# Criss-cross attention on one core: the second pair of channel tiles takes rows first and columns second, with a head of 30 projection pieces and no turn

## What is computed

```python
q = einsum('bchw,oc->bohw', x, Wq) + bq      # 64 channels, k alike
v = einsum('bchw,oc->bohw', x, Wv) + bv      # 512 channels
eH = einsum('bchw,bcpw->bhwp', q, k)         # column strip, diagonal masked with -inf
eW = einsum('bchw,bchp->bhwp', q, k)         # row strip
att = softmax(concat([eH, eW], 3), 3)
outH = einsum('bcpw,bhwp->bchw', v, att[..., :H])
outW = einsum('bchp,bhwp->bchw', v, att[..., H:])
out = gamma * (outH + outW) + x
```

## Time and profile before

| | |
|---|---|
| median of 3 runs | 4426.95 us (4395.76 to 4439.74) |
| the profiled execution: time, span | 4430.1 us, 4428.3 us |
| share of the span in which PE, DVE, ACT, POOL are busy | 80%, 58%, 42%, 28% |
| mean granted TensorE clock, as a share of full | 0.86 |
| moved by DMA | 1179.35 MB, mean 266 GB/s |

### The profile page before, as it was taken

One profiled execution on the slowest core, in us unless ns is written; L12 is line 12 of the kernel. 1 busy time (PEld: TensorE's weight loads), 2 busy tenths in 40 slices (PEclk: granted clock), 3 DMA queues, 4 the chain that ended last, 5 costly groups with the idle time before them and its releaser, 6 DMA issues.

```text
span 4428.3 us, 97049 instructions
## 1 busy us (share of the span) xinstructions
PE 3545.5 (80%) x33624; PEld 2431.6 (55%) x33624; DVE 2586.0 (58%) x3802; ACT 1875.7 (42%) x3852; POOL 1246.6 (28%) x1075
## 2 busy tenths in 40 slices
PE   3987978778887887878977798878988778884865
PEld 1544755456564564645655466554755456563755
DVE  6546764477554774538745576455765477554643
ACT  1545634165241752427532474325634165242621
POOL 0000341404413044220433214240241404413333
PEclk9998799888898798997999879889799888996665
DMA  7958688986989779996899968899689986999399
GB/s 273 297 187 276 209 275 263 326 279 197 312 259 315 255 200 307 289 315 224 240 303 310 302 206 257 273 325 292 208 272 268 330 280 194 316 261 286 96 288 287
DMA packets 824051, 1179.35 MB, mean 266 GB/s; under 512 B 56560, under 2 KB 574192, under 8 KB 823536
## 3 DMA queue, kind: packets, MB, share of 16 engines
q1 hardware_dynamic: 509136, 831.94, 61.5%
q10 hardware_dynamic: 314400, 340.86, 24.0%
HBM read 832.83 MB, written 339.74 MB: 265 GB/s over the span
## 4 chain that ended last, share of the span: by engine, by line
issue 33%; DMA 26%; PE 21%; POOL 10%; DVE 4%; SPq 3%; ACT 2%; ACTq 1%; POOLq 0%; DVEq 0%
DMA xr<-x 23%; POOL acc L496 4%; PE banks L1033 4%; PE banks L1034 4%; PE banks L1035 4%; POOL prob_col L486 4%; PE banks L1107 3%; PE banks L1109 2%; PE banks L1108 2%; DMA v_in<-v_pixel_major 2%; POOL qk_pair L468 2%; SPq L377 1%; DVE floor L770 1%; PE banks L1085 1%; DMA x_first<-x 1%
## 5 line engine op out<-in xcount | busy, mean ns | idle before, releaser
L1033 PE MATMUL banks<-wv_hi,x_hi 128*128 128x512 f16 x2304 | 936.2, 406 | 247.9 <-DVE x_lo L804 247.8
L812 DVE SCALAR_TENSOR_TENSOR v_out<-banks,proj,v_out 128x512 f16<-128x512 f32 x576 | 431.2, 749 | 1076.7 <-ACT v_out L591 1075.8
L496 POOL TENSOR_TENSOR acc<-acc,xr 128x768 f32<-128x768 f32 x384 | 716.3, 1866 | 878.0 <-DMA xr<-x 700.5
L1034 PE MATMUL banks<-wv_lo,x_hi 128*128 128x512 f16 x2304 | 930.1, 404 | 0.0
L1035 PE MATMUL banks<-wv_hi,x_lo 128*128 128x512 f16 x2304 | 924.5, 401 | 0.0
L591 ACT ACTIVATE v_out<-banks,proj 128x512 f16<-128x512 f32 x576 | 390.8, 684 | 970.3 <-PE banks L1035 968.9
L468 POOL TENSOR_TENSOR qk_pair<-qk_f,qk_pair 128x256 f16<-128x256 f32 x288 | 202.6, 703 | 2034.4 <-ACT qk_pair L607 2027.2
L1107 PE MATMUL banks<-prob_row,v_in 96*128 96x96 f16 x3072 | 475.0, 217 | 309.9 <-DMA v_in<-v_pixel_major 259.9
L893 DVE SCALAR_TENSOR_TENSOR acc<-banks,att,acc 128x384 f32<-128x384 f32 x768 | 443.1, 609 | 266.6 <-PE banks L1109 265.9
L1033 PEld LDWEIGHTS banks<-wv_hi,x_hi 128*128 128x128 f16 x2304 | 237.6, 103 | 519.7 <-issue 314.7
L1107 PEld LDWEIGHTS banks<-prob_row,v_in 96*128 96x128 f16 x3072 | 318.8, 104 | 367.0 <-issue 229.6
(11 more groups left out here) (104 smaller groups left out, 7055.4 us busy)
## 6 DMA issues: line engine op xcount, KB each, us to landing
v_in<-v_pixel_major SPq DMA_DIRECT2D x768, 384.0 KB, 7.1
x_raw<-x ACTq DMA_DIRECT2D x290, 512.0 KB, 6.9
x_next<-x SPq DMA_DIRECT2D x384, 384.0 KB, 3.7
v_pixel_major<-v_out ACTq DMA_DIRECT2D x576, 256.0 KB, 4.0
xr<-x SPq DMA_DIRECT2D x384, 384.0 KB, 9.5
out<-acc SPq DMA_DIRECT2D x384, 384.0 KB, 8.6
qk_halves<-qk_pair ACTq DMA_DIRECT2D x288, 128.0 KB, 4.1
x_first<-x SPq DMA_DIRECT2D x24, 768.0 KB, 9.0
```

What stands on the lines that cost most here:

```text
L496: nc.gpsimd.tensor_tensor(acc[tt][:, px], acc[tt][:, px], xr[n % XR][:, :], ALU.add).then_inc(res_added, 1)
L812: nc.vector.scalar_tensor_tensor(out=v_out[tile % V_OUT][:, :, 1, :], in0=bank[tile % 2][:, :].rearrange("p (t c) -> p t c", t=CT), scalar ...
L1033: nc.tensor.matmul(dst, s_hi, m_hi, start=(t == 0), stop=False)
L1034: nc.tensor.matmul(dst, s_hi, m_lo, start=False, stop=False)
```

## The change

Four edits go together.

- The second pair of channel tiles takes its rows first and its columns second. The first pass of a pair overwrites the accumulator, whatever its direction (`evacuate_first`), and the second is added (`add_second`), now also for columns.
- The residual of the second pair is added in its first pass, chunk by chunk as the rows come. Before the first column add, DVE waits for all of them.
- The chunks of the second pair are no longer stored one by one: SP waits for the last column add and then issues all 24 stores. For the first pair nothing changes.
- The wait for the first pair's stores is now one per chunk, at the row group that overwrites the chunk. The turn goes, and its 10 items move to the head: HEAD is 30. The two halves of groups still lie over 30 items each.

```diff
-    HEAD = 20
+    HEAD = 30
     STATS = 6
-    TURN = 10
     S_ITEMS = HEAD + NP + STATS
     T_ITEMS = ITEMS - S_ITEMS
-    DEAL = (T_ITEMS - TURN) // 2
+    DEAL = T_ITEMS // 2
...
         def group_at(i):
-            return i // HALF, (COL, ROW)[i // (NG * TT) % 2], i // TT % NG, i % TT
+            tp = i // HALF
+            return tp, ((COL, ROW), (ROW, COL))[tp][i // (NG * TT) % 2], i // TT % NG, i % TT
...
+            def finish(b, g):
+                tp, o, h, tt = group_at(g)
+                if o == ROW and h % 2:
+                    if tp == 0:
+                        sp.wait_ge(res_added, b * CHUNKS + chunk_number(g) + 1 + XR)
+                        store_chunk(b, tp, h // 2, tt)
+                    n = chunk_number(g) + XR
+                    if n < (tp + 1) * (TT * NCH):
+                        load_residual(b, n)
...
-                    if g % HALF == HALF // 4:
+                    if g == HALF // 4 or g == HALF:
                         for n in range(XR):
-                            load_residual(b, g // HALF * (TT * NCH) + n)
+                            load_residual(b, tp * (TT * NCH) + n)
...
+                wait_alone(sp, second_added, (b + 1) * (GROUPS // 2) + ONE0)
+                for c in range(NCH):
+                    for tt in range(TT):
+                        store_chunk(b, TP - 1, c, tt)
...
-            def evacuate_column(b, g):
+            def evacuate_first(b, g):
...
-                if h == 0 and tp > 0:
-                    for c in range(NCH):
-                        wait_alone(dve, out_stored[tt][c], b * (TP * 16) + tp * 16 + 16)
+                if h % 2 == 0 and tp > 0:
+                    wait_alone(dve, out_stored[tt][h // 2], b * (TP * 16) + tp * 16 + 16)
...
-            def add_row(b, g):
+            def add_second(b, g):
...
+                if o == COL and h == 0 and tt == 0:
+                    wait_alone(dve, res_added, (b + 1) * CHUNKS + XR)
                 dve.wait_ge(o_mm, b * GROUPS + g + 1 + ONE0)
-                a = acc_strips[tt][ROW][:, h * G:(h + 1) * G, :]
+                a = acc_strips[tt][o][:, h * G:(h + 1) * G, :]
```

More of the change, by code:

```diff
@@ L252, in criss_cross_attention @@
         o_mm = sem("o_mm")
-        col_act = sem("col_act")
-        col_dve = sem("col_dve")
-        row_added = sem("row_added")
+        first_act = sem("first_act")
+        first_dve = sem("first_dve")
+        second_added = sem("second_added")
         xr_loaded = [sem(f"xr_loaded{u}") for u in range(XR)]
@@ L313, in groups_after @@
                 return range(k, k + 1)
[L314 to L317, removed]
+            return range(k * HALF // DEAL, (k + 1) * HALF // DEAL)
         block = ctx.enter_context(nc.Block())
@@ L695, in batch @@
                             high_parts(b, g // TT + AHEAD)
-                        if o == COL and tt == 0:
-                            evacuate_column(b, g)
+                        if not is_second(g) and tt == 0:
+                            evacuate_first(b, g)
                 if items:
@@ L875, in evacuate_column @@
                     wait_alone(dve, factor_row_ready, b + 1)
-                if h == 0 and tp > 0:
-                    for c in range(NCH):
-                        wait_alone(dve, out_stored[tt][c], b * (TP * 16) + tp * 16 + 16)
+                if h % 2 == 0 and tp > 0:
+                    wait_alone(dve, out_stored[tt][h // 2], b * (TP * 16) + tp * 16 + 16)
                 dve.wait_ge(o_mm, b * GROUPS + g + 1 + ONE0)
                 nc.vector.tensor_scalar(
-                    acc_strips[tt][COL][:, h * G:(h + 1) * G, :], out_bank[g % OUTS], att[:, O_FACTOR:O_FACTOR + 1],
+                    acc_strips[tt][o][:, h * G:(h + 1) * G, :], out_bank[g % OUTS], att[:, O_FACTOR:O_FACTOR + 1],
                     gbv_col[:, tp * TT + tt:tp * TT + tt + 1], ALU.mult, ALU.add,
-                ).then_inc(col_dve, 1)
-            def add_row(b, g):
+                ).then_inc(first_dve, 1)
+            def add_second(b, g):
                 tp, o, h, tt = group_at(g)
                 if h == 0 and tt == 0:
-                    wait_alone(dve, col_act, b * (TP * NG) + (tp + 1) * NG + ONE0)
+                    wait_alone(dve, first_act, b * (TP * NG) + (tp + 1) * NG + ONE0)
                 if h == 0 and tt == 1:
-                    wait_alone(dve, col_dve, b * (TP * NG) + (tp + 1) * NG + ONE0)
+                    wait_alone(dve, first_dve, b * (TP * NG) + (tp + 1) * NG + ONE0)
+                if o == COL and h == 0 and tt == 0:
+                    wait_alone(dve, res_added, (b + 1) * CHUNKS + XR)
                 dve.wait_ge(o_mm, b * GROUPS + g + 1 + ONE0)
-                a = acc_strips[tt][ROW][:, h * G:(h + 1) * G, :]
+                a = acc_strips[tt][o][:, h * G:(h + 1) * G, :]
                 nc.vector.scalar_tensor_tensor(
```

76 lines of the change are left out of this document (35 added, 41 removed).

## The result

The changed kernel takes 4546.66 us (median of 4 runs, 4542.7 to 4561.84), the kernel before 4429.26 us beside it (4 runs, 4395.76 to 4439.74). The ratio is 1.0294, with a 95% interval of 1.0245 to 1.0344: slower by 2.9%. The forecast was 4595 us within 4465 to 4710.

A forecast was written before the change was run, and what follows sets the result against it. No engine full: transfers bind the head and both row stages, DVE the scores, PE the second columns. Six batches at +21, batch 0 at -6 and the last at +45 give +165 on 4430.1: 4595 us, range 4465 to 4710.

The forecast's parts named there:

- The head: Start of a batch: 24 stores and ten more items add 13.4 MB, 38 us at 350 GB/s, bounds 24 to 43.
- the share of 1.03: DMA share over the whole head at 309 GB/s, read as showing that stage bound by transfers.
- Rival A: Head and rows cost less: stores fill gaps, head +24 us, residual pace 2.8, column add 0.94; 4445 us, chance 0.15.
- Rows of the second pair: After the residual drain: 21 us start, then 20 chunks at 3.1 us, 83 us in all (77 to 99).
- Rival D: New waits cost more: PE stopped for residuals, DVE's items stuck behind; rows 99 us, +16 a batch, 4710 us, chance 0.08.
- Columns of the second pair: Last stage turns from PE's to DVE's: 48 adds at 1.0 us, 17 of items, 3 of waits: 68 us (60 to 81).
- rival C: Faster: unmixed reads and writes, head +24 us, second rows at PE's pace; 4404 us, 4350 if columns stay at 60; chance 0.07.
- the upper bound of 1.28 us: DVE's column add in the second pair, if strided reading and writing are both paid; column stage then 81 us.
- Rival B: Column add pays twice, 1.28 us: 13 us more in seven batches and the last; 4700 us, chance 0.10.
- Scores, first columns, first rows: Middle stages of a batch keep their items and groups: no change.
- Batch 0: First batch, no stores ahead of its head: 11 us more there, 17 gained later, -6 us.
- The last batch: No items hide anything: first score +22 us, from first pair's residuals to the end +23, together +45 us.

The follow-up runs named there:

- small stores: Kernel before, each second-pair chunk storing only its first 16 columns; 4355.94 us, a batch 7.5 us shorter.
- the small residuals: Changed kernel, second pair's residual loads bringing only the first 16 columns of each chunk; 4326.91 us.
- The head alone: Kernel before with a head of 30 items and no turn, its order of rows and columns kept; 4422.69 us, ratio 1.0013.
- the order alone: Changed kernel with the old head of 20 items and turn of 10 restored; 4589.9 us, ratio 1.0388.
- 8/22: Kernel before, 8 items in each column stage and 22 in each row stage instead of 15 and 15; 4338.36 us, ratio 0.9818.
- 12/18: Kernel before, 12 items in each column stage and 18 in each row stage instead of 15 and 15; 4414.93 us, ratio 0.9983.
- 11/19: Kernel before, 11 items in each column stage and 19 in each row stage instead of 15 and 15; 4505.07 us, ratio 1.021.
- with the head of 30 the dealing that had won: Kernel before with a head of 30, no turn, and items dealt 8 / 22 / 8 / 22; 4460.44 us, ratio 1.0104.

## Why the prediction was right, and which of its steps were wrong

**Sign, size and the place of the loss** held: a batch grew by 13.4 us where I had 21, the last one most of all. But several terms were off, and part of them cancelled, so that the total is nearer than the terms: that part is luck.

**The head: +30.5 instead of +38, for another reason.** I had 27 us for the stores and 11 for ten items, all by bytes. The runs show 25 for the items and 6 to 7 for the stores in this head. The failed step is the sentence that takes the share of 1.03 as a bound by bytes: the stage was bound by PE and the loads of x behind it, and the 24 us that I kept as a lower bound "if the stores cost nothing and the ten items come at PE's rate" was the truth for the items. The first score came at 89.4 us, for 99.

**Stores hide behind loads.** Rival A's mechanism ("the stores fill gaps") was nearly right in the head (30.5 us for its 24), and wrong in the rows, where it had the pace fall to 2.8.

**Rows of the second pair: 96.1 instead of 83 us.** The start was as costed (18.6 us of 21), the pace was not: 3.87 us a chunk, where I took 3.1 and had 3.9 as the case in which the pace stays. The step that failed counted all bytes alike, 1.43 MB down to 1.03. What was removed was a write, and the writes were not what the chain waited for: without stores in the old order it fell by 0.42 us only. The chain waits for its loads, and it loads more a chunk here (0.91 MB) than it did in the old order (0.76, with small stores). Rival D had 99 us, near the measured time, but by new waits of PE; the small residuals show that it is the loads.

**Columns of the second pair: 60.4 instead of 68 us.** The add's duration was costed well (0.956 for 1.0 us), but the records of adds in a row overlap: 48 of them keep DVE busy for 42.7 us, 0.89 each, and the whole stage has 54.4 us where I had 48 + 17 = 65. Of the difference 7 us are overlap of records, of the items' as well, and the rest is that adds and items were each some 2 us shorter in sum. Beside it stand 6 us of waits for my 3. The step that failed is to take the mean duration of a record for the time that the next one waits. The groups of that stage:

```profile
L901 DVE SCALAR_TENSOR_TENSOR acc<-banks,att,acc 128x384 f32<-128x384 f32 x48 | 42.7, 982 | 13.2 <-POOL acc L504 13.1
L819 DVE SCALAR_TENSOR_TENSOR v_out<-banks,proj,v_out 128x512 f16<-128x512 f32 x9 | 6.8, 754 | 6.3 <-ACT v_out L599 6.3
L811 DVE SCALAR_TENSOR_TENSOR x_lo<-x_raw,proj,x_hi 128x1024 f16<-128x1024 f32 x4 | 5.3, 1316 | 0.0
L828 DVE TENSOR_SCALAR qk_f<-banks,proj 128x256 f32<-128x256 f32 x5 | 2.9, 582 | 0.0
```

The 13.1 us of waiting for POOL in the first row are those ahead of the first add, the wait that the change brought. "I am wrong if the column stage stays at 60": it did, as rival C had it; that rival's rows at PE's pace did not come, so the gain stayed away. By the page "SBUF — State Buffer" of the Trainium skill ("Door 1: the DMA port swizzle"), as I read it, the upper bound of 1.28 us would have been the value. The direction is as it says (956 against 604 ns), but the add pays 352 ns, and not twice the 263 that the overwrite pays. Rival B falls with it.

**Handover:** 5.5 us for 5. Together pair 2 took 162.2 us from the 24th residual to the next batch, for my 156; before, 172.0 in the mean, for the 173 of the one batch that I read.

**Scores, first columns, first rows: -7.3 instead of 0.** I had "keep their items and groups". The head alone gives the same -7.5, the order alone gives +19.1 (17.3 of it in the scores, by x_next), so this part goes with the head of 30: the items of these stages are ten further on in the next batch's work. At 8/22 the same shift cost 10.6 us instead. What exactly in the items does it is open; the size, 5 to 10 us either way, is what an item plan moves here without any byte or instruction more.

**Batch 0: +6.2 instead of -6.** It has no stores, but its head grew by 22.7 us, the items' price, for which I had 11, a miss of 12 us and as large as the whole one; two others cancel, 5.5 us less up to the 24th residual where I had no change, and 11 us gained behind it for my 17. **The last batch: +29 instead of +45.** Head 15.2 for 22, rows 82.5 for 75, columns 40.9 for 51, stores 26 for 30. Its columns, which have no items beside them:

```profile
4476.00:4517.00 41.00, 29.98 (x540) 26.01 (x540) 39.47 (x47) 0.00 (x0) 1.10 (x1) 0.92 0.78 184
```

DVE is busy 39.5 of 41 us with 47 adds, 840 ns each. Here DVE does bind, as I had it for every batch.

**Sum.** My batch: 38 - 17 = 21. Measured: 30.5 - 9.8 - 7.3 = 13.4.

## What to carry to other kernels

A DMA share near 1 doesn't say that bytes bind: look at the rate of loads and stores apart, and ask which of them the chain waits for. Removing stores from a stage that waits for its loads gives a third of their bytes' time or less. Price moved work by the engine that does it as well as by its bytes, take the larger, and look for the stages where the loads bind: that is where PE's work can be nearly free (here 1.8% of the whole for two numbers). Measure it, though: in the same kernel 12/18 gave nothing and 11/19 lost 2.1%, and with the head of 30 the dealing that had won lost 0.9% (1.0104 for 1.0013).

## What the runs showed of the hardware

- Loads of residuals, v and x ran, by the transfer records, at 235 GB/s in the second rows of the changed kernel (last 20 chunks, mean of six batches), at 224 in the old order with small stores, and at about 200 beside the stores of the kernel before; loads of x, q and k ran at 240 in the changed kernel's head (1446 to 1483). With stores the total was 320 and 330 to 370 GB/s. A residual packet of 3 KB took 181 ns (median) in the changed kernel's second rows.
- The Trainium skill's page "DMA: Bandwidth & Descriptors" ("Bandwidth") has 425 GB/s for one transfer of 16 MB. The nearest here are the first loads of x at 390 GB/s, 370 GB/s while 24 stores ran beside items, and 363 GB/s for the stores alone.
- A column-order access (steps of 384 bytes, 384 elements) costs DVE's overwrite 263 ns over its 676 and its add 352 ns over its 604.
- 24 stores with 16 columns each still take 13.3 us alone at the end of the last batch, against 26 for 9.44 MB.
